# Moving the two normalising activations ahead of the attention-output copy on ScalarE

## The chip, the cores and the metric

The kernel runs on one core of one Trainium2 chip. The metric is the device time of one execution in microseconds (us); lower is better. Engines are called by their short names: PE is TensorE (matmuls, with PEld for the loading of weights), DVE is VectorE, ACT is ScalarE, POOL is GpSimd, SP is SyncE.

## The reference, cut to what matters

A gated cross-attention block followed by a top-1 mixture of experts, over 128 sequences of 128 tokens with 256 features, 16 heads of 16 features, 8 experts:

```python
x = x + tanh(g_xattn[0]) * xattn(layernorm(x), ctx, ctx, bias, ...)   # bias: (128, 16, 128, 128)
x = x + tanh(g_ffn[0])   * ffn(layernorm(x), Wg, bg, W1, b1, W2, b2)

# xattn, one sequence: q, k, v = projections with a low-rank addition
scores = einsum('bqhd,bkhd->bhqk', q * D**-0.5, k) + bias
out = einsum('bhqk,bkhd->bqhd', softmax(scores), v)
# ffn: expert = argmax(x @ Wg + bg); y = gelu(x @ W1[e] + b1[e]) @ W2[e] + b2[e]
```

Each sequence therefore needs two layer norms: one of the input x before the attention, and one of the attention's result (called x2 here) before the expert layer.

## The kernel before, in words

There are two stages. The first works through the 128 sequences, one step k for each, and ends with every token's normalised row scattered to its expert's list in memory. The second runs the expert layer on 72 tiles of 256 tokens. The change lies in the first.

The first stage is a software pipeline written out by hand, separately for each engine. In step k each engine handles several sequences at different ages. The names in the code say which: `nxt` is sequence k+4 (its input is normalised and transposed), `val` k+3 (values), `qry` k+2 and `ky` k+1 (queries and keys, each in every second step for two sequences at once), `cur` k (scores, bias, row maximum), `prev` k-1 (transposing of the scores and the exponentials), `fin` k-2 (probabilities times values, and the output's transpose back), `old` k-3 (second layer norm, transpose of x2), `gate` k-4 and `grp` k-5 (routing, once for four sequences). Eight steps form the body of a hardware loop that runs for k = 16 to 119; the steps before and after are written out.

Each engine executes its instructions in the order in which they are written, and semaphores tie the engines together. In step k:

* PE: scores of `cur` (L464); routing logits in every fourth step (L507); probabilities times values of `fin` into bank 6, `b_x` (L516); eight transposes of `prev` (L479, quarters 0 and 1); then it waits for the copy OT (semaphore `ot_evac`, L529) and transposes OT back (L531); small routing matmuls in some steps (L534, L537, L538); queries or keys (L486), values (L564, L566), the transpose of the normalised x2 (L577), the transposes of the normalised x and of the context (L588, L591) and the other eight transposes of `prev` (L479).
* DVE: in every fourth step `pick_experts` (L863 to L879) and in the step after it `list_slots` (L885 to L891); then two bias additions (L829), a row maximum (L835), two more additions, a second maximum; then, once OT's transpose is done (`o_ready`), the normalisation by the softmax sum, x2 (L928), and the statistics of the two layer norms. The last instruction of the step's statistics is L858 for x2.
* POOL: subtracts the maxima (L381, two a step), and then turns the statistics into a scale and a shift: L400, a power (L402) and two small L407, the first for x, the second for x2. Each L407 signals `shift_ok`. Then it scatters one sequence's rows (L416).
* ACT: the order is that of the diff: in every fourth step the copy LT; the copy OT of bank 6 (L699); the two `normalise` calls (L678, first x2 of `old`, then x of `nxt`), which wait for `shift_ok`; the exponentials of quarters 0 and 1 of `prev` (L685); queries or keys (L658, L669), the copies V (L715), x2T (L721) and XT (L728), and the exponentials of quarters 2 and 3.

The scale and shift that ACT uses in step k come from statistics that DVE finished at the end of step k-1.

I call the four kinds of step by their place in a group of four: A is k mod 4 = 3 (routing logits), B is k mod 4 = 0 (DVE's `pick_experts`), C is 1 (DVE's `list_slots`), D is 2 (nothing extra).

Of the kernel before, what the change touches and what calls it, by code (L numbers as in the profile page):

```python
# [88 lines left out]
def run_steps(eng, first, last, width, loop_rounds, body, heads=None):  # L89

    a, b = loop_rounds
    for s in range(first, a * width):
        body(0, s)
    with eng.bass.Fori(a, b, engines=bass.OrderedEngineSet([eng.engine]), head_slot=heads) as i:
        for k in range(width):
            body(i, k)
    for s in range(b * width, last + 1):
        body(0, s)


def flamingo_block(nc, x, ctx_in, bias, g_xattn, g_ffn, wqT, bq, aq, bqT, wkT, bk, ak, bkT, wvT, bv, av, bvT,
                   wg, bg, w1, w2, b2, consts, row_consts, ids_const, out):
    ctx = ExitStack()
    with ctx:
        def sb(name, shape, dt=F32):
            return ctx.enter_context(nc.sbuf_tensor(name, shape, dt))

        def sem(name):
            return ctx.enter_context(nc.semaphore(name))
# [32 lines left out]
        x_sb = sb("x_sb", [P, 8, HID])  # L142
        ctx_sb = sb("ctx_sb", [P, 4, HID])
        sc = sb("sc", [P, 4, HEADS * P])
        xn = sb("xn", [P, 2, HID])
# [10 lines left out]
        xn2, x2id = x2n[:, :, 0:HID], x2n[:, :, HID]  # L156
        ln = x2n[:, :, HID + 1:HID + 9].rearrange("p t (n c) -> p t n c", c=4)
        x2 = sb("x2", [P, 2, HID])
# [61 lines left out]
        ve_ok, rs_ok, xn_ok, xn2_ok = (sem(t) for t in ("ve_ok", "rs_ok", "xn_ok", "xn2_ok"))  # L220
        shift_ok = [sem(f"shift_ok{i}") for i in range(2)]
        xt_ready, xt_evac = sem("xt_ready"), sem("xt_evac")
# [8 lines left out]
        x2t_ready, x2t_evac = sem("x2t_ready"), sem("x2t_evac")  # L231
# [32 lines left out]
        def seq(i, k, lag):  # L264

            t = At(i, k - lag, U)
            if isinstance(i, int) and not 0 <= i * U + k - lag < N:
                return None
            return t

        def tile(i, k, lag):
            t = At(i, k - lag, FU)
            if isinstance(i, int) and not 0 <= i * FU + k - lag < TILES:
                return None
            return t
# [367 lines left out]
        @block.scalar  # L643
        def _(act):
            for w, wt, a, b in (("v", wvT, av, bvT), ("q", wqT, aq, bqT), ("k", wkT, ak, bkT)):
                act.dma_start(A[w][:], a).then_inc(s_w[w], 16)
                act.dma_start(B[w][:], b).then_inc(s_w[w], 16)
                act.dma_start(W[w][:], wt).then_inc(s_w[w], 16)
            act.wait_ge(s_g, 16 * FIRST_DMAS)
            nc.scalar.activation(tg[:], g_raw[:], ACT.Tanh).then_inc(s_seta, 1)  # L650

            def queries(t):
                pair = t.k // 2 % 2
                if t.reached(4):
                    act.wait_ge(s_ready, t.n(4, -8))
                for o in range(KC):
                    act.wait_ge(q_ready, t.per(2, KC, o + 1))
                    ins = nc.scalar.activation(QT[:, pair, o, :], b_s[o][:, 0:2 * P],  # L658
                                               ACT.Identity, bias=bq_col[:, o:o + 1])
                ins.then_inc(q_evac, 1)  # L660

            def keys(t):
                pair = t.k // 2 % 2
                if t.reached(4):
                    act.wait_ge(s_ready, t.n(4, -8))
                for o in range(KC):
                    act.wait_ge(k_ready, t.per(2, KC, o + 1))
                    for e in range(2):
                        ins = nc.scalar.activation(  # L669
                            KT[:, pair, o, :, e, :], b_s[o][:, 0:2 * P].rearrange("p (s k) -> p s k", s=2),  # L670
                            ACT.Identity, bias=bk_half[:, e, o:o + 1], scale=half_rows[e])
                ins.then_inc(k_evac, 1)

            def normalise(t, n, row, rows, dst, done, turned):
                act.wait_ge(shift_ok[n], t.n(1, 1))
                if t.reached(2):
                    act.wait_ge(turned, t.n(1, -1))
                nc.scalar.activation(dst, rows, ACT.Identity, bias=ln[:, row, n, 1:2],  # L678
                                     scale=ln[:, row, n, 0:1]).then_inc(done, 1)

            def probs(t, q):
                act.wait_ge(tr_ready, t.n(4, q + 1))
                if q == 0 and t.reached(2):
                    act.wait_ge(ot_ready, t.n(1, -1))
                nc.scalar.activation(PT[:, t.slot(2), 512 * q:512 * q + 512], b_t[q % 2][:],  # L685
                                     ACT.Exp).then_inc(pt_ready, 1)

            def step(i, k):
                nxt, val, qry, ky, prev, fin, old, gate = (seq(i, k, lag) for lag in (-4, -3, -2, -1, 1, 2, 3, 4))
                if gate and gate.slot(4) == 3:  # L690
                    act.wait_ge(lt_ready, gate.per(4, 1, 1))
                    if gate.reached(4):
                        act.wait_ge(l_ok, gate.per(4))
                    nc.scalar.copy(LT[:], b_lt).then_inc(lt_evac, 1)
                if fin:
                    act.wait_ge(ot_ready, fin.n(1, 1))
                    if fin.reached(1):
                        act.wait_ge(o_ready, fin.n())
                    nc.scalar.copy(OT[:], b_x[:]).then_inc(ot_evac, 1)  # L699
                if old:  # L700
                    normalise(old, 1, (k - 3) % 8, x2[:, old.slot(2), :], xn2[:, old.slot(8), :], xn2_ok, x2t_ready)
                if nxt:
                    normalise(nxt, 0, (k - 3) % 8, x_sb[:, nxt.slot(8), :], xn[:, nxt.slot(2), :], xn_ok, xt_ready)
                if prev:
                    probs(prev, 0)
                    probs(prev, 1)
                if qry and qry.slot(2) == 0:
                    queries(qry)
                if ky and ky.slot(2) == 0:
                    keys(ky)  # L710
                if val:
                    act.wait_ge(v_ready, val.n(1, 1))
                    if val.reached(8):
                        act.wait_ge(ot_ready, val.n(1, -7))
                    nc.scalar.copy(V[:, val.slot(8), :, 0:D],  # L715
                                   b_v[:, 0:HID].rearrange("p (h d) -> p h d", d=D)).then_inc(v_evac, 1)
                if old:
                    act.wait_ge(x2t_ready, old.n(1, 1))
                    if old.reached(8):
                        act.wait_ge(lt_ready, old.per(4, 1, -1))  # L720
                    nc.scalar.copy(x2T[:, old.slot(8)], b_x2[:, 0:HID].rearrange("p (c t) -> p c t", t=P)  # L721
                                   ).then_inc(x2t_evac, 1)
                if nxt:
                    pair, tok = nxt.k // 2 % 2, P * nxt.slot(2)
                    act.wait_ge(xt_ready, nxt.n(1, 1))
                    if nxt.reached(4):
                        act.wait_ge(k_ready, nxt.per(2, KC, -KC))
                    nc.scalar.copy(XT[:, pair, :, tok:tok + P],  # L728
                                   b_x[:].rearrange("p (c t) -> p c t", t=P)).then_inc(xt_evac, 1)
                if prev:  # L730
                    probs(prev, 2)
                    probs(prev, 3)

            run_steps(act, FIRST, LAST, U, LOOP, step)

            def fstep(i, k):
                t = tile(i, k, -1)
                if t:
                    act.wait_ge(gt_ready, t.n(1, 1))
                    if t.reached(2):  # L740
                        act.wait_ge(h_ready, t.n(1, -1))
                    nc.scalar.copy(xgT[:, t.slot(2)], bank[t.slot(2)][:].rearrange("p (c t) -> p c t", t=FT)  # L742
                                   ).then_inc(gt_evac, 1)
                t = tile(i, k, 0)
                if t:
                    act.wait_ge(h_ready, t.n(1, 1))
                    if t.reached(2):
                        act.wait_ge(y_ready, t.n(1, -1))
                    for o in range(KC):
                        ins = nc.scalar.activation(hT[:, t.slot(2), o, :],  # L750
                                                   bank[2 + t.slot(2)][:, FT * o:FT * o + FT], ACT.Gelu,
                                                   bias=w1_sb[:, t.slot(4), KC * HID + o:KC * HID + o + 1])
                    ins.then_inc(h_ok, 1)

            run_steps(act, FFIRST, FLAST, FU, FLOOP, fstep)
# [326 lines left out]
```

## Time and profile before

| | |
|---|---|
| median of 3 runs | 1427.01 us (1424.8 to 1427.34) |
| the profiled execution: its own time, its span | 1427.01 us, 1424.8 us |
| PE busy | 1359.5 us, 95% |
| PE weight loads busy | 1145.5 us, 80% |
| DVE busy | 1077.0 us, 76% |
| POOL busy | 962.4 us, 68% |
| ACT busy | 895.4 us, 63% |
| granted TensorE clock, mean | 0.981 |

The span runs from the first to the last instruction; the time of a run is 2.2 us longer than it here. The first stage is busy from about 33 us (scores of step 0) to about 1085 us, the expert stage from about 1110 us to the end. In the hardware loop the pattern repeats itself: from the second round on, each round of eight steps lasts 65.4 us to within 0.05 us. Busy time on PE is modelled for each matmul and neighbouring matmuls overlap, so the starts of the groups tell more than the sums.

### The profile page before, as it was taken

The numbers are of one execution on the slowest core, as the hardware profiler recorded it, in microseconds if no ns is written. First come the engines' busy times: TensorE is split into PE (matmuls) and PEld (weight loads), VectorE is DVE, ScalarE is ACT, GpSimd is POOL, SyncE is SP. The second block draws the span as 40 slices with busy tenths as digits, with TensorE's granted clock in tenths as the row PEclk, the third lists the DMA queues.
The fourth block names the chain that finished last, engine by engine and source line by source line (L and its number), as shares of the span: only waits on it lengthen the run. The fifth ranks groups of instructions, "written<-read, shape, count | busy, mean of one in ns | idle before, by whom it ended". The sixth has DMA issues, their size and how long they took to land.

```text
span 1424.8 us, 43541 instructions
## 1 busy us (share of the span) xinstructions
PE 1359.5 (95%) x13462; PEld 1145.5 (80%) x13462; DVE 1077.0 (76%) x2591; ACT 895.4 (63%) x1915; POOL 962.4 (68%) x1062
## 2 busy tenths in 40 slices
PE   6999999999999999999999999999993789999997
PEld 4788888888888888888888888888873678888886
DVE  4899899888889898998898898988996233333333
ACT  2677777777777777777777777777762323333332
POOL 3667777777777777777777777777775234444444
PEclk7999999999999999999999999999996899999999
DMA  7466566665665565666666655666631788888883
GB/s 200 127 171 178 169 187 178 175 187 168 178 187 164 171 191 167 183 183 171 185 173 172 193 164 167 190 172 178 186 106 44 239 248 274 258 260 261 256 254 117
DMA packets 350771, 264.79 MB, mean 186 GB/s; under 512 B 18007, under 2 KB 313335, under 8 KB 350714
## 3 DMA queue, kind: packets, MB, share of 16 engines
q1 hardware_dynamic: 337130, 228.61, 57.5%
q0 software_dynamic: 13056, 34.63, 6.5%
q10 hardware_dynamic: 528, 0.84, 0.2%
q8 instruction: 30, 0.49, 0.1%
q14 instruction: 27, 0.22, 0.1%
HBM read 226.88 MB, written 39.22 MB: 187 GB/s over the span
## 4 chain that ended last, share of the span: by engine, by line
PE 42%; DVE 23%; issue 18%; ACT 9%; POOL 3%; SPq 2%; DMA 1%; DVEq 1%; POOLq 0%; ACTq 0%
DVE sc L829 9%; PE bank L637 8%; PE bank L623 8%; PE bank L479 5%; PE bank L486 5%; ACT PT L685 4%; PE bank L464 3%; PE bank L516 3%; PE bank L566 2%; ACT KT L669 2%; PE bank L612 2%; DVE st L850 2%; DVE x L928 2%; POOL x2n L402 2%; DVE negmax L835 2%
## 5 line engine op out<-in xcount | busy, mean ns | idle before, releaser
L381 POOL TENSOR_TENSOR sc<-sc,negmax 128x1024 f32<-128x1024 f32 x256 | 484.9, 1897 | 126.5 <-DVE negmax L835 122.3
L829 DVE TENSOR_TENSOR sc<-bank,sc 128x512 f32<-128x512 f32 x512 | 328.2, 682 | 49.7 <-PE bank L464 42.8
L835 DVE TENSOR_REDUCE negmax<-sc 128x8 f32<-128x1024 f32 x256 | 312.3, 1220 | 17.0
L685 ACT ACTIVATE PT<-bank 128x512 f32<-128x512 f32 x512 | 277.5, 599 | 0.2
L479 PE MATMUL bank<-cst,sc 128*128 128x128 f32 x2048 | 273.4, 277 | 0.0
L433 POOL DMA_INDIRECT out<-og,ids x144 | 141.7, 984 | 179.3 <-issue 156.5
L479 PEld LDWEIGHTS bank<-cst,sc 128*128 128x128 f32 x2048 | 226.1, 141 | 25.7 <-issue 25.5
L994 DVE SCALAR_TENSOR_TENSOR og<-bank,tg,sc 128x512 f32<-128x512 f32 x72 | 54.1, 751 | 194.2 <-PE bank L637 186.9
L416 POOL DMA_INDIRECT rows_dram<-x2n,slot_i x128 | 138.6, 1083 | 59.1 <-issue 55.2
L699 ACT COPY OT<-bank 128x512 f32<-128x512 f32 x128 | 75.1, 587 | 151.0 <-PE bank L516 151.0
L464 PE MATMUL bank<-KT,QT 32*128 32x256 f32 x2048 | 146.6, 400 | 2.4 <-issue 1.6
L516 PE MATMUL bank<-PT,V 128*32 128x128 f32 x4096 | 138.4, 276 | 6.4 <-ACT PT L685 5.4
L637 PE MATMUL bank<-sc,hT 128*128 128x256 f32 x576 | 144.2, 380 | 0.0
L623 PE MATMUL bank<-xgT,w_sb 128*128 128x256 f32 x576 | 138.0, 383 | 5.4 <-ACT xgT L742 4.4
L516 PEld LDWEIGHTS bank<-PT,V 128*32 128x32 f32 x4096 | 107.1, 110 | 40.4 <-ACT PT L685 36.1
L566 PE MATMUL bank<-wv,XT 128*128 128x256 f32 x512 | 132.6, 382 | 0.0
L486 PE MATMUL bank<-XT,wq 128*128 128x256 f32 x512 | 125.8, 389 | 2.7 <-DVE sc L829 2.0
L486 PE MATMUL bank<-XT,wk 128*128 128x256 f32 x512 | 124.5, 386 | 0.4 <-DVE sc L829 0.4
L669 ACT ACTIVATE KT<-bank,bk_half,cst 128x256 f32<-128x256 f32 x256 | 123.4, 567 | 1.0
L742 ACT COPY xgT<-bank 128x512 f32<-128x512 f32 x72 | 42.1, 585 | 130.0 <-PE bank L612 130.0
L623 PEld LDWEIGHTS bank<-xgT,w_sb 128*128 128x128 f32 x576 | 104.6, 192 | 19.0 <-ACT xgT L742 5.2
L750 ACT ACTIVATE hT<-bank,w_sb 128x256 f32<-128x256 f32 x144 | 60.4, 470 | 91.8 <-PE bank L623 91.8
(134 smaller groups left out, 2217.1 us busy)
## 6 DMA issues: line engine op xcount, KB each, us to landing
sc<-in_bias SPq DMA_DIRECT2D x256, 512.0 KB, 5.0
xg<-rows_dram SPq DMA_DIRECT2D x72, 272.0 KB, 3.6
w_sb<-in_w SPq DMA_DIRECT2D x72, 257.0 KB, 4.1
sc<-in_w SPq DMA_DIRECT2D x72, 256.0 KB
x_sb<-in_x SPq DMA_DIRECT2D x128, 128.0 KB, 2.1
ctx_sb<-in_ctx_in SPq DMA_DIRECT2D x128, 128.0 KB, 4.9
rows_dram<-vacant SPq DMA_DIRECT2D x9, 272.0 KB, 3.1
out<-og,ids POOLq DMA_INDIRECT x144
```

Source lines behind the costliest of these rows:

```text
L381: nc.gpsimd.tensor_tensor(s, s, m, ALU.add).then_inc(sub_ok, 1)
L464: ins = mm(b_s[j][:, 2 * P * c:2 * P * c + 2 * P], QT[rows, pair, c, P * sq:P * sq + P], KT[rows, pair, c, sq].rearrange("p e k -> p (e k) ...
L479: ins = nc.tensor.transpose(b_t[q % 2][:, P * h:P * h + P], sc[:, t.slot(4), o:o + P], ident)
L486: ins = mm(b_s[o][:, 0:2 * P], W[w][:, c, o * P:o * P + P], XT[:, t.k // 2 % 2, first + c, :], start=(c == 0), stop=(c == KC - 1))
L516: ins = mm(b_x[CELL * j:CELL * j + CELL, P * (h // 4):P * (h // 4) + P], V[:, fin.slot(8), h, :], PT[:, fin.slot(2), P * h:P * h + P], sta ...
L566: ins = mm(b_v[:, 0:HID], XT[:, pair, KC + c, tok:tok + P], W["v"][:, c, :], start=False, stop=(c == KC - 1))
L623: ins = mm(bank[2 + t.slot(2)][:, FT * o:FT * o + FT], w1_sb[:, t.slot(4), c * HID + o * P:c * HID + o * P + P], xgT[:, t.slot(2), c, :], ...
L637: ins = mm(y_half, hT[:, t.slot(2), c, a * P:a * P + P], w2_sb[:, t.slot(4), c * HID:c * HID + HID], start=False, stop=(c == KC - 1))
L669: ins = nc.scalar.activation(KT[:, pair, o, :, e, :], b_s[o][:, 0:2 * P].rearrange("p (s k) -> p s k", s=2), ACT.Identity, bias=bk_half[:, ...
L685: nc.scalar.activation(PT[:, t.slot(2), 512 * q:512 * q + 512], b_t[q % 2][:], ACT.Exp).then_inc(pt_ready, 1)
L829: nc.vector.tensor_tensor(s, b_s[q][:], s, ALU.add).then_inc(s_used, 1)
L835: nc.vector.tensor_reduce(negmax[:, t.slot(2), 8 * h:8 * h + 8], sc[:, t.slot(4), 1024 * h:1024 * h + 1024].rearrange("p (h k) -> p h k", ...
```

## The change

In ACT's step the two `normalise` calls are moved from behind the copy OT to ahead of it. Nothing is added or removed: the same instructions with the same waits, in another order on this one engine's queue.

```diff
                 if gate and gate.slot(4) == 3:
...
                     nc.scalar.copy(LT[:], b_lt).then_inc(lt_evac, 1)
+                if old:
+                    normalise(old, 1, (k - 3) % 8, x2[:, old.slot(2), :], xn2[:, old.slot(8), :], xn2_ok, x2t_ready)
+                if nxt:
+                    normalise(nxt, 0, (k - 3) % 8, x_sb[:, nxt.slot(8), :], xn[:, nxt.slot(2), :], xn_ok, xt_ready)
                 if fin:
                     act.wait_ge(ot_ready, fin.n(1, 1))
                     if fin.reached(1):
                         act.wait_ge(o_ready, fin.n())
                     nc.scalar.copy(OT[:], b_x[:]).then_inc(ot_evac, 1)
-                if old:
-                    normalise(old, 1, (k - 3) % 8, x2[:, old.slot(2), :], xn2[:, old.slot(8), :], xn2_ok, x2t_ready)
-                if nxt:
-                    normalise(nxt, 0, (k - 3) % 8, x_sb[:, nxt.slot(8), :], xn[:, nxt.slot(2), :], xn_ok, xt_ready)
                 if prev:
                     probs(prev, 0)
                     probs(prev, 1)
```

## Rows read from the trace of the kernel before

**Rows 1.** Windows: busy PE, PEld, DVE, ACT, POOL; granted clock, DMA share, GB/s.

```profile
617.48:682.87 65.39, 65.03 (x742) 55.16 (x741) 58.70 (x136) 49.29 (x107) 50.53 (x56) 1.00 0.62 177
158.90:160.40 1.50, 0.00 (x0) 0.00 (x0) 0.92 (x6) 0.69 (x2) 1.14 (x3) 1.00 0.55 127
1085.00:1110.00 25.00, 5.01 (x30) 3.54 (x30) 12.65 (x41) 1.24 (x3) 9.48 (x10) 0.50 0.21 69
```

**Rows 2.** Waits in that loop round: total us, times, longest.

```profile
ACT OT L699 <- PE bank L516: 9.2, 8, 1.5
...
PE bank L516 <- ACT PT L685: 0.3, 1, 0.3
```

**Rows 3.** Timeline of PE, one group of four steps: start, duration.

```profile
642.08 1.15 PE L464 MATMUL bank<-KT,QT 32*128 32x256 f32 x16
...
645.53 0.60 PE L531 MATMUL bank<-cst,OT 128*128 128x128 f32 x4
...
650.51 1.15 PE L464 MATMUL bank<-KT,QT 32*128 32x256 f32 x16
...
653.53 0.60 PE L531 MATMUL bank<-cst,OT 128*128 128x128 f32 x4
...
658.74 1.15 PE L464 MATMUL bank<-KT,QT 32*128 32x256 f32 x16
...
661.76 0.60 PE L531 MATMUL bank<-cst,OT 128*128 128x128 f32 x4
...
666.52 1.15 PE L464 MATMUL bank<-KT,QT 32*128 32x256 f32 x16
...
674.43 1.15 PE L464 MATMUL bank<-KT,QT 32*128 32x256 f32 x16
675.50 0.64 PE L507 MATMUL bank<-x2T,wg_pad 128*32 128x128 f32 x16
```

**Rows 4.** Timeline of ACT in two steps of kind C.

```profile
629.43 0.60 ACT L678 ACTIVATE x2n<-x,x2n 128x256 f32<-128x256 f32 x1 [0.62 <-POOL x2n L407]
...
660.96 0.59 ACT L699 COPY OT<-bank 128x512 f32<-128x512 f32 x1 [1.42 <-PE bank L516]
661.79 0.60 ACT L678 ACTIVATE x2n<-x,x2n 128x256 f32<-128x256 f32 x1 [0.24 <-POOL x2n L407]
662.30 0.59 ACT L678 ACTIVATE xn<-x_sb,x2n 128x256 f32<-128x256 f32 x1
662.79 1.05 ACT L685 ACTIVATE PT<-bank 128x512 f32<-128x512 f32 x2
```

**Rows 5.** Timeline of DVE: first additions of a step, last statistics.

```profile
617.27 0.18 DVE L858 BATCH_NORM_AGGREGATE mv<-st 128x2 f32<-128x6 f32 x1
...
620.10 1.29 DVE L829 TENSOR_TENSOR sc<-bank,sc 128x512 f32<-128x512 f32 x2 [0.23 <-DVE CNT L879]
...
627.27 0.18 DVE L858 BATCH_NORM_AGGREGATE mv<-st 128x2 f32<-128x6 f32 x1
...
643.24 1.29 DVE L829 TENSOR_TENSOR sc<-bank,sc 128x512 f32<-128x512 f32 x2 [1.00 <-PE bank L464]
...
650.31 0.18 DVE L858 BATCH_NORM_AGGREGATE mv<-st 128x2 f32<-128x6 f32 x1
...
652.63 0.69 DVE L829 TENSOR_TENSOR sc<-bank,sc 128x512 f32<-128x512 f32 x1 [0.21 <-DVE CNT L879]
...
659.70 0.18 DVE L858 BATCH_NORM_AGGREGATE mv<-st 128x2 f32<-128x6 f32 x1
```

**Rows 6.** Timeline of POOL, the same group: scale and shift.

```profile
661.26 0.50 POOL L407 TENSOR_SCALAR x2n<-x2n,mv 128x1 f32<-128x1 f32 x2 [0.18 <-POOL x2n L402]
```

**Rows 7.** Timeline at the end of the first stage.

```profile
1080.34 0.58 ACT L699 COPY OT<-bank 128x512 f32<-128x512 f32 x1 [1.20 <-PE bank L516]
...
1081.04 0.42 PEld L531 LDWEIGHTS bank<-cst,OT 128*128 128x128 f32 x4 [1.04 <-issue]
...
1087.51 1.08 PE L507 MATMUL bank<-x2T,wg_pad 128*32 128x128 f32 x16 [0.46 <-ACT x2T L721]
```

## The prediction

> **What bounds the kernel now.** I read the windows first. One round of the loop is eight steps in 65.39 us, of which PE is busy 65.03 us; DVE has 58.70, POOL 50.53, ACT 49.29 [rows 1]. Busy time on PE is modelled, so I checked it in the timeline of PE: its groups follow each other without a hole, and the group of four steps from 642.08 to 674.43 takes 32.35 us (8.43 in A, 8.23 in B, 7.78 in C, 7.91 in D) [rows 3]. So PE sets the pace of the first stage, with little to spare. In the list of waits ACT's largest in that round is the one of the copy OT for PE's L516: 9.2 us in eight waits [rows 2]. ACT is idle there, about 1.2 us a step, and that is the hole into which the change could move 1.0 us of work. Whether it can depends on when that work is allowed to start, and on how soon PE wants OT after it. So the views that decide are the timelines of the four engines around one copy.
>
> **What the two sides of the copy allow.** In step C the copy runs from 660.96 to 661.55 [rows 4] and PE starts the transpose of OT at 661.76 [rows 3]. PE would have to wait for a copy that ended later than that, less the hand-over. The hand-over from OT's end to PE is seen where PE did wait: OT ended at 1080.92, PE's weight load began at 1081.04, 0.12 us later [rows 7]. So the copy has 661.76 - 661.55 - 0.12 = 0.09 us of slack.
>
> The `normalise` calls wait for POOL's shift. It was ready only at 661.26 + 0.50 = 661.76 [rows 6], and the first of them started at 661.79, after the copy, having kept ACT idle for 0.24 us; in the C step of the other group it was 0.62 us [rows 4]. They are thus in their present place not late because they stand behind OT, but because of POOL and, ahead of it, DVE.
>
> **The change step by step.** In the new order OT starts behind both. From the end of DVE's last statistics to the first activation: 661.79 - (659.70 + 0.18) = 1.91 us here, and 629.43 - (627.27 + 0.18) = 1.98 us in the other group [rows 4, 5]. Then 0.51 us to the second activation and 0.49 us to the next instruction (here an activation that reads the same kind of bank, so I take it for OT), 0.59 us of the copy [rows 4], and 0.12 us to PE. From the end of the statistics of step k-1 to PE's L531 of step k that makes 3.62 us (3.69 in the other group).
>
> With the statistics where they are now, C's L531 would start at 659.88 + 3.62 = 663.50 instead of 661.76, 1.74 us later; in B at 650.49 + 3.62 = 654.11 instead of 653.53, 0.58 us later [rows 3, 5]. That is a new wait of PE in nearly every step. Behind it on PE's queue stand the projections, the transposes and the next scores; DVE's next additions wait for those scores. The order of ACT's later work hardly matters: the exponentials follow OT by 0.5 us instead of 1.5 us.
>
> The waits don't add up in full, for DVE and POOL gain on a PE that is late. The new pace is that of the longest closed loop of dependences. I follow it through one group, beginning at the late L531 of C:
>
> * PE from L531 of C to the scores of D: 666.52 - 661.76 = 4.76 us [rows 3].
> * PE through D: 7.78 us, taken from C, the step of the same work that did not wait (D's own 7.91 holds a short wait for an exponential) [rows 3].
> * scores of A to DVE's first addition: 643.24 - 642.08 = 1.16 us [rows 3, 5].
> * DVE through A: 643.24 to 650.49, 7.25 us without a hole; `pick_experts` to the first addition of B, 652.63 - 650.49 = 2.14 us; DVE through B to 659.88, 7.25 us [rows 5].
> * hand-over to C's L531: 3.62 us.
>
> Sum: 33.96 us a group, against 32.35 now. In the other group, the one at the start of a loop round, DVE takes 620.10 - 617.45 = 2.65 us for `pick_experts` and 627.45 - 620.10 = 7.35 us for B [rows 5], and the hand-over is 3.69: 34.64 us. The round is then 68.60 us instead of 65.39 [rows 1]: 3.2 us more in eight steps, 0.40 us a step.
>
> Do the other waits add to this loop? Let A start at 0. D took 7.78 us and its statistics ended at most 1.16 + 7.25 us after its start, so 0.63 us into A. A's L531 is then at 0.63 + 3.62 = 4.25 instead of 3.45 (645.53 - 642.08 [rows 3]): up to 0.8 us late. A's statistics end at 8.41. B starts 4.98 us after A's L531 (650.51 - 645.53), at 9.23, and its own L531 could be had 8.41 + 3.62 - 9.23 = 2.80 us into it, before its present 3.02: no wait. B's statistics end at 8.41 + 2.14 + 7.25 = 17.80, C starts at 9.23 + 8.23 = 17.46, and its L531 is 3.96 us into it instead of 3.02: 0.9 us late. The same sum with 2.65, 7.35 and 3.69 gives 1.6 us in the other group. D starts at 26.18, C's statistics end at 17.46 + 1.16 + 7.25 = 25.87 at the latest, and D's L531 is 0 to 0.3 us late; I count nothing for it. So the waits sit in A and C, and the one in A is not on the loop, since DVE doesn't wait for PE in B.
>
> Thirteen rounds of the loop: 13 x 3.2 = 41.7 us. The 24 other steps of the stage have the same order of work; at 0.4 us each 9.6 us. The expert stage is untouched: 0. Total +51 us. Against the profiled execution's own 1427.01 us, which is the median of the runs, that gives 1478 us.
>
> **Bounds.** Low: hand-overs 0.1 us shorter in each group and 0.2 us of DVE's pace gained (1.4 us a group), and nothing in the 24 other steps: 13 x 2.8 = 36, 1463 us. High: each of four hand-overs 0.15 us longer (2.2 us a group) in all 32 groups, 70 us: 1497 us. I take the middle, since every term is a start-to-start distance in the trace. The likeliest case's own range is 1463 to 1497.
>
> **Rivals.** (a) *No catching up.* If every late L531 counted in full, B and C would lose 0.58 + 1.74 = 2.3 us. For D and A I have no such pair of rows; with nothing for them it is 32 x 2.3 = 74 us, with as much again 148 us; I take the upper, as D's statistics follow C's late ones: 1575 us. It needs DVE to be as late as PE at every wait; but DVE takes up OT's transpose only behind its four additions and two maxima, and the loop above shows it running through A and B without PE. Chance 0.04.
>
> (b) *Hidden.* PE's stall is absorbed, no change, 1427 us. That needs a slack of 1 us a step on PE, or statistics that come 0.6 us ahead of every step now; they come 0.02 us ahead of B and 1.14 us after the start of C [rows 3, 5]. Against a slack speaks that PE's starts are dense; for it, that its weight loads fill only 55.16 of 65.39 us [rows 1]. Chance 0.05. The Trainium skill (Perfetto Trace Analysis, Identifying the Most-Contended Engine) says that matmul occupancy does not tell how close TensorE is to its limit and that the busy share of weight loading should be used. By that rule PE has 16% to spare and the sum would be 0 instead of +51; by the dense starts it is +51, and the starts are what the next engine waits for.
>
> (c) *The other side: faster.* Once the activations are out of the way, the exponentials come 1 us sooner behind OT, and PE's wait for them goes: 0.3 us in one step of the round [rows 2] and 0.1 us in D. 0.4 us in 16 rounds' worth of steps is 6 us, 1421 us. It decides if the shift is ready by the time that ACT falls idle, 1.2 us or more before L516 ends, so if the statistics end 0.6 us before each step starts; the rows put them at or after it. Chance 0.03.
>
> (d) *The clock.* The granted clock is 1.00 in the loop and 0.50 between the stages, where PE does 5.01 us of work in 25; a single pause of 1.5 us left it at 1.00 [rows 1]. The new waits are 0.8 to 1.6 us, twice a group. At the lower level, 1.2 GHz, L507 takes 1.08 us instead of 0.64 [rows 3, 7]. If one step in four ran so, 7.8 x 0.69 = 5.4 us a group would come on top: 1478 + 32 x 5.4 = 1651 us. Chance 0.03. The Trainium skill (TensorE: Matmul & The Clock Gate, A second HAM failure mode: psum-queue depth-cycling) tells of a kernel whose frequent short idles between groups made the clock swing between the two levels; by it this case would be the likely one, by the pause in the trace it is not.
>
> **How the numbers follow.** Forecast 0.85, (a) 0.04, (b) 0.05, (c) 0.03, (d) 0.03. A measurement of this kernel can tell 0.2% from no change. Slower holds the forecast, (a) and (d), 0.92; same is (b), 0.05; faster (c), 0.03. The range 1463 to 1497 holds nearly all of the forecast's 0.85, so it stands as it is, with 1460 and 1500 as round ends.
>
> **What the profile would show.** A round of eight steps of 68.6 us. L531 held back by OT in A (up to 0.8 us) and C (0.9 and 1.6 us) and hardly in B and D. ACT's wait of OT for L516 gone, and in its place a wait of the first normalising activation for POOL in every step. DVE waiting for PE's scores in D and A. The clock at 1.00. The prediction is wrong if L531 doesn't wait, if it waits in all four kinds (then (a)), or if the matmuls themselves get longer (then (d)).

## The result and the profile after

The changed kernel takes 1483.49 us (median of 4 runs, 1481.97 to 1484.63) against 1427.17 us for the kernel before beside it. The ratio is 1.0392, 95% interval 1.0377 to 1.0407: 3.9% slower. The forecast was 1478 us, within 1460 to 1500.

| | before | after |
|---|---|---|
| span of the profiled execution | 1424.8 us | 1480.4 us |
| granted TensorE clock, mean | 0.981 | 0.981 |
| one loop round, eight steps | 65.39 us | 68.76 us |
| its steps B C D A, first group | 8.52, 7.95, 8.13, 8.43 | 8.22, 9.56, 7.79, 9.10 |
| its steps B C D A, second group | 8.23, 7.78, 7.91, 8.44 | 8.23, 8.89, 7.84, 9.11 |

The steps are distances between the starts of PE's scores. The windows view of one round of the changed kernel answers to the first row of [rows 1]; columns as there:

```profile
579.15:647.89 68.74, 65.29 (x741) 55.00 (x740) 58.82 (x137) 49.92 (x107) 50.56 (x57) 1.00 0.59 169
```

Every engine does the work it did before; only the length of the round grew, and the clock stayed at 1.00. The waits in the same round (total us, times, longest) answer to [rows 2]:

```profile
ACT x2n L678 <- POOL x2n L407: 6.0, 8, 2.2
DVE sc L829 <- PE bank L464: 5.3, 5, 2.1
...
PE bank L531 <- ACT OT L703: 3.4, 4, 1.6
```

ACT's 9.2 us of waiting for L516 are gone. In their place the first activation waits for POOL's shift, eight times in eight steps, and behind it PE waits for OT in four of the eight: 3.4 us, about what the round grew by. DVE in its turn waits for PE.

The timelines of PE through A, B and C of the second group, and of DVE and ACT in its C (start, duration, the idle time ahead and what ended it) answer to [rows 3, 4, 5]:

```profile
604.72 1.15 PE L464 MATMUL bank<-KT,QT 32*128 32x256 f32 x16
608.78 0.66 PE L531 MATMUL bank<-cst,OT 128*128 128x128 f32 x4 [0.45 <-ACT OT L703]
613.82 1.15 PE L464 MATMUL bank<-KT,QT 32*128 32x256 f32 x16
616.84 0.60 PE L531 MATMUL bank<-cst,OT 128*128 128x128 f32 x4
622.05 1.15 PE L464 MATMUL bank<-KT,QT 32*128 32x256 f32 x16
626.15 0.63 PE L531 MATMUL bank<-cst,OT 128*128 128x128 f32 x4 [0.93 <-ACT OT L703]
630.94 1.15 PE L464 MATMUL bank<-KT,QT 32*128 32x256 f32 x16
```

```profile
622.35 0.18 DVE L858 BATCH_NORM_AGGREGATE mv<-st 128x2 f32<-128x6 f32 x1
```

```profile
624.45 0.60 ACT L678 ACTIVATE x2n<-x,x2n 128x256 f32<-128x256 f32 x1 [1.59 <-POOL x2n L407]
624.95 0.59 ACT L678 ACTIVATE xn<-x_sb,x2n 128x256 f32<-128x256 f32 x1
625.45 0.56 ACT L703 COPY OT<-bank 128x512 f32<-128x512 f32 x1
```

L531 is held in A (4.06 us after the scores instead of 3.45) and in C (4.10 instead of 3.02), and not in B. In C the statistics ended at 622.35 + 0.18 = 622.53 and L531 began at 626.15: 3.62 us, the hand-over of the prediction to the last digit. In the C of the first group L531 is held longest, 4.77 us after the scores instead of 3.02:

```profile
587.37 1.15 PE L464 MATMUL bank<-KT,QT 32*128 32x256 f32 x16
592.14 0.63 PE L531 MATMUL bank<-cst,OT 128*128 128x128 f32 x4 [1.59 <-ACT OT L703]
```

The chain of work that ended last shows the closed loop itself, here from B of the first group into the next A (start, length, engine and line; the longest pieces only):

```profile
578.76 0.20 DVE lmax L863
...
581.70 0.69 DVE sc L829
...
588.27 0.19 DVE mv L858
588.62 0.24 POOL ve L400
588.93 0.73 POOL x2n L402
590.06 0.27 POOL x2n L407
590.95 0.58 ACT xn L678
591.53 0.48 ACT OT L703
592.14 0.63 PE bank L531 x4
592.77 1.73 PE bank L486 x8
...
597.00 1.08 PE bank L464 x16
...
600.12 0.44 PE bank L531 x4
...
604.78 1.11 PE bank L464 x16
...
606.49 0.69 DVE sc L829
```

`pick_experts` and the rest of DVE's B, POOL, ACT, PE's L531 in C, PE through D to the scores of A, and DVE again. The L531 of D (600.12) lies on it as PE's work, not as a wait.

### The profile page after: what moved, and what is told of

The parts are those of the page before. It is cut to its first block, busy times and chain, and to the rows that moved or that the text cites. A ratio compares the mean times of both kernels' runs of the same rounds, so it can differ in the third digit from the quotient of the medians.

```text
span 1480.4 us, 43554 instructions
## 1 busy us (share of the span) xinstructions
PE 1367.4 (92%) x13462; PEld 1144.0 (77%) x13462; DVE 1079.3 (73%) x2591; ACT 904.5 (61%) x1915; POOL 962.8 (65%) x1062
## 4 chain that ended last, share of the span: by engine, by line
PE 48%; DVE 23%; issue 17%; ACT 3%; POOL 3%; SPq 3%; DVEq 1%; DMA 1%; POOLq 0%; ACTq 0%
DVE sc L829 9%; PE bank L486 8%; PE bank L637 7%; PE bank L623 7%; PE bank L479 6%; PE bank L464 5%; PE bank L566 4%; PE bank L531 2%; PE bank L516 2%; DVE st L850 2%; PE bank L612 2%; DVE x L928 2%; POOL x2n L402 2%; DVE negmax L835 2%; DVE CNT L879 2%
## 5 line engine op out<-in xcount | busy, mean ns | idle before, releaser
L416 POOL DMA_INDIRECT rows_dram<-x2n,slot_i x128 | 138.6, 1083 | 59.0 <-issue 55.1
L678 ACT ACTIVATE x2n<-x,x2n 128x256 f32<-128x256 f32 x128 | 77.0, 601 | 106.6 <-POOL x2n L407 105.7
L516 PE MATMUL bank<-PT,V 128*32 128x128 f32 x4096 | 137.6, 275 | 1.8 <-ACT PT L685 1.8
L531 PE MATMUL bank<-cst,OT 128*128 128x128 f32 x512 | 79.7, 278 | 58.0 <-ACT OT L703 58.0
L516 PEld LDWEIGHTS bank<-PT,V 128*32 128x32 f32 x4096 | 106.5, 110 | 33.9 <-ACT PT L685 29.5
```

Source lines behind the costliest of these rows:

```text
L516: ins = mm(b_x[CELL * j:CELL * j + CELL, P * (h // 4):P * (h // 4) + P], V[:, fin.slot(8), h, :], PT[:, fin.slot(2), P * h:P * h + P], sta ...
```

## The experiments

Ratios are against the kernel before on the same chip, whose time there was 1433 to 1436 us; so ratios are compared, not times. The round lengths are the distances between PE's scores in each timeline, once the pattern repeats. They are set beside the 65.39 us of the kernel before, whose only trace comes from the chip of the main comparison, where it took 1427 us; no trace shows its rounds on the chips of the experiments. The new line numbers of the variants are shifted by up to four.

**The wait alone.** Both activations stay behind OT; OT only has to wait for the shift.

```diff
+                if fin and old:
+                    act.wait_ge(shift_ok[1], old.n(1, 1))
                 if fin:
                     act.wait_ge(ot_ready, fin.n(1, 1))
```

> The order of the kernel before, with one wait added: OT waits for the shift of x2 (shift_ok) before it copies; both activations stay behind it. My theory (closed loop PE - DVE A - DVE B - POOL - ACT - PE): the hand-over from the statistics to L531 is 1.91 + 0.59 + 0.12 = 2.62 us, so the groups take 33.0 and 33.7 us, a round of eight steps 66.6 instead of 65.4, in all +19 us: 1446 us (1440 to 1452). Rival W (it is the 1.0 us of ACT's work ahead of the copy that costs, whatever it waits for): nothing, 1427 us. Rival of the first order (each late L531 counts in full, 0.7 us in C and 0.5 in D, none in A and B): also about +20 to +40, so it is told apart by the place: by my theory L531 waits in C alone or nearly so.

Ratio 1.0103 (1.0083 to 1.0122), +15 us (+19 expected); a round 66.65 us, steps of the groups 8.51, 8.88, 7.78, 8.44 and 8.24, 8.57, 7.79, 8.45: only C is longer. The round is as the sum had it (66.6). So a wait without any work moved costs a quarter of the change.

**The work alone.** Two activations of the same size that wait for nothing, at the head of ACT's step.

```diff
+                if fin:
+                    act.wait_ge(s_cst, 16)
+                    for c in range(KC):
+                        nc.scalar.activation(hT[:, 0, c, :], cst[:, 0:FT], ACT.Identity,
+                                             bias=minus_half, scale=minus_half)
                 if gate and gate.slot(4) == 3:
```

> The order of the kernel before, with two additional activations of the same size (128x256, scale and bias from a column) at the head of ACT's step, which wait for nothing and write a buffer that nobody reads in this stage; 2 x 0.5 us more work of ACT ahead of every copy OT. My theory: they fit into the hole in which ACT waits for L516 (1.15 us a step), so nothing: 1427 us (1424 to 1433). Rival W (ACT's work ahead of the copy is the cost): +1 us in every step less what catches up, about as the change itself, 1483 us.

Ratio 0.9997 (0.9987 to 1.0007). 1.0 us more of ACT's work ahead of each of 128 copies costs nothing against the kernel before on the same chip: it fills the idle stretch. That ends the rival W here: what costs is that the work ahead of the copy has to wait for the shift. (Its profiled round was 65.86 us, 0.5 longer than in the trace of the kernel before; more on that below.)

**Each half of the change.** With only the activation for x ahead of OT:

> The other half: only the activation for x stands ahead of OT, the one for x2 stays behind it. Its shift is the first of the two that POOL writes, some 0.25 us earlier. My theory: hand-over 2.87 us, groups 33.2 and 33.9, a round 67.1 us, in all +27 us: 1454 us (1448 to 1460), so less than with x2 alone. Rival W: the same as with x2 alone, 1455 us for both.

Ratio 1.0156 (1.0136 to 1.0177), +22 us (+27 expected), a round 67.13 us, as the sum had it (67.1). With only the one for x2:

> Half of the change: only the activation for x2 stands ahead of OT, the one for x stays behind it. My theory: the hand-over is 1.91 + 0.49 + 0.59 + 0.12 = 3.11 us instead of 3.62, the groups take 33.45 and 34.13, a round 67.6 us, in all +35 us: 1462 us (1457 to 1468), that is clearly more than half of the change's +56. Rival W: half of the change, 1455 us.

Ratio 1.0349 (1.0329 to 1.0370), +50 us. Its rounds are uneven, 67.3 to 70.4 us, with a mean of 68.9; the one read here took 69.41 us where the sum gave 67.6. One activation fewer ahead of OT, and rounds as long as in the full change (68.76). This miss needed a cause of its own. Its timeline, ACT and then PE in a step D, shows it:

```profile
529.02 0.60 ACT L678 ACTIVATE x2n<-x,x2n 128x256 f32<-128x256 f32 x1 [0.64 <-POOL x2n L407]
530.83 0.59 ACT L701 COPY OT<-bank 128x512 f32<-128x512 f32 x1 [1.21 <-PE bank L516]
```

```profile
528.65 1.08 PE L516 MATMUL bank<-PT,V 128*32 128x128 f32 x32
529.66 1.09 PE L479 MATMUL bank<-cst,sc 128*128 128x128 f32 x8
531.47 0.66 PE L531 MATMUL bank<-cst,OT 128*128 128x128 f32 x4 [0.72 <-ACT OT L701]
```

ACT is free from 529.62, L516 ends at 529.73, and OT starts at 530.83: 1.1 us in which nothing that it waits for is open. POOL's row of the same moment:

```profile
529.46 1.08 POOL L416 DMA_INDIRECT rows_dram<-x2n,slot_i  x1 [0.48 <-issue]
```

**Is it the order of OT's waits?** OT waits for two semaphores. In this one the one for `o_ready` is taken at the head of ACT's step, ahead of the activation for x2.

> The kernel with x2's activation alone ahead of OT was 15 us slower than my sum, and its trace shows OT up to 1.1 us after L516 with ACT idle. Here the wait for o_ready stands at the head of the step instead of at OT. If the lateness comes from OT's two waits being taken up one after the other behind the waiting activation, it goes, and the round is 67.6 us (the kernel some +35 us against before). If it is something else, the time stays at about +50 us.

1487.72 us (one run), 53 us above the kernel before beside it, rounds of 69.44 us: the lateness stays, so it is not that.

**The power left out.** On POOL:

```diff
                     nc.gpsimd.tensor_tensor(ln[:, row, a:b, 0], ve[:, a:b], minus_half.broadcast_to([P, b - a]),
-                                            ALU.pow).then_inc(rs_ok, 1)
+                                            ALU.mult).then_inc(rs_ok, 1)
```

> The changed kernel with POOL's power (0.72 us) replaced by a multiplication of the same operands; the output is no longer the reference's, since the layer norm's scale is wrong. It shortens the hand-over by what POOL saves, I expect 0.3 to 0.5 us. My theory: the hand-over is on the closed loop once a group, so a round gets 0.6 to 1.0 us shorter and the kernel 10 to 16 us faster than the changed one: ratio to the kernel before 1.028 to 1.032 instead of 1.039. Rival W (ACT's work is the cost): no gain beyond what the kernel before gains by the same edit.

> The kernel before with the same replacement of the power (output not the reference's, as in the other). My theory: POOL's hand-over is not on PE's path there, only ACT's two waits for the shift in a round get shorter and with them up to 0.4 us of PE's waits a round: ratio 0.996 to 1.000, clearly less gain than in the changed kernel.

POOL's L402 fell from 0.72 to 0.20 us, and both expectations failed: 1.0334 (1.0317 to 1.0350) for the changed kernel, and for the kernel before 1.0201 (1.0184 to 1.0219), 2% slower by doing less. In the first the ratio is lower than the change's 1.0392, but the rounds are not shorter: 68.4 to 69.5 us, 68.9 in the mean, against 68.76. The kernel before was slower on this chip, and that lowers the ratio. The second has the same mark as above: OT up to 1.1 us after L516, now in the old order, with ACT idle for long. The timeline of PE, POOL and ACT in an A:

```profile
596.09 1.06 PE L516 MATMUL bank<-PT,V 128*32 128x128 f32 x32
596.84 1.04 POOL L416 DMA_INDIRECT rows_dram<-x2n,slot_i  x1 [0.39 <-issue]
598.17 0.58 ACT L699 COPY OT<-bank 128x512 f32<-128x512 f32 x1 [1.49 <-PE bank L516]
```

L516 had ended at 597.15, and POOL's scatter had begun 0.31 us before.

I went through OT's copies in all these timelines (those between 160 and 1010 us). A scatter is early if POOL's L416 began more than 0.08 us before L516 ended. A copy is late if it came more than 0.2 us after both L516 and ACT's own last work allowed it. The fifth column counts the clearest cases: ACT was idle and waiting when L516 ended, and the scatter had begun 0.08 to 1.2 us before; the sixth says how many of these copies were late. The last column is the time of the kernel before on the same chip. The wait alone is left out, since its copies wait for the shift too.

| kernel | copies | scatter early | copy late | both | waiting, scatter early | of these late | kernel before there |
|---|---|---|---|---|---|---|---|
| before | 104 | 11 | 0 | 0 | 10 | 0 | 1427 us |
| changed | 99 | 49 | 0 | 0 | 12 | 0 | 1427 us |
| x2 alone ahead | 98 | 50 | 42 | 40 | 17 | 17 | 1434 us |
| x alone ahead | 101 | 2 | 2 | 2 | 2 | 2 | 1434 us |
| work alone | 104 | 25 | 25 | 25 | 25 | 25 | 1434 us |
| x2 alone, `o_ready` first | 98 | 58 | 47 | 47 | 22 | 22 | 1435 us |
| before, no power | 100 | 74 | 65 | 65 | 61 | 61 | 1435 us |
| changed, no power | 98 | 84 | 62 | 62 | 37 | 37 | 1435 us |
| both behind the exponentials (below) | 105 | 1 | 1 | 1 | 1 | 1 | 1435 us |

In the clearest cases the copy was late 165 times out of 165 in seven variants, and 0 times out of 22 in the kernel before and the changed one. That is the split between the chips: these two kernels were profiled where the kernel before takes 1427 us, all variants where it takes 1433 to 1436 us. The split may therefore belong to the chip and not to the kernels. It isn't shown, since neither of the two was profiled on the variants' chips, and no variant on theirs.

A shift that is ready earlier lets the scatter go earlier, and on those chips an earlier scatter goes with late copies. So I tested whether it is their cause.

**The scatter held.** POOL waits for the L516 that OT waits for before it scatters; nothing else changes. (POOL's work behind the scatter moves with it; in the late copy shown above POOL's next work begins only after the copy does.)

```diff
+                    held = seq(i, k, 1)
+                    if held:
+                        pool.wait_ge(ot_ready, held.n(1, 1))
+                        pool.nop(nofuse=True)
                     g, j = t.k // 4 % 2, t.slot(4)
                     nc.gpsimd.indirect_dma_start(
```

> The kernel with x2's activation alone ahead of OT cost 49 us where my sum gave 35, and its trace shows copies OT that start up to 1.1 us after L516 although nothing they wait for is open; that happens where POOL's scatter L416 began before L516 ended. Here POOL waits for L516 of the sequence two behind before it scatters, so that L416 begins only after L516. If the scatter is what delays the copy: no late copies, a round of 67.6 us, ratio to the kernel before 1.024 (1.021 to 1.028). If it is something else: ratio 1.035 as without the hold.

Ratio 1.0222 (1.0205 to 1.0239), a round 67.64 us, no late copy in 100. The windows view of a round, with the hold and without it:

```profile
501.67:569.31 67.64, 65.19 (x741) 54.94 (x740) 58.66 (x136) 49.85 (x107) 50.62 (x57) 1.00 0.60 172
```

```profile
509.61:579.02 69.41, 65.95 (x742) 54.95 (x741) 58.77 (x136) 50.12 (x107) 50.54 (x56) 1.00 0.58 167
```

The sum for this order was 67.6 us. The miss was the scatter's, not the loop's.

> The kernel before without the power (output not the reference's) was 2.0% slower, against my sum; its shift is ready 0.5 us earlier and so is the scatter, which then falls ahead of L516's end. With the scatter held until L516 is done: if the scatter is the cause, ratio 0.996 to 1.001, as my theory had it for this edit; if not, 1.020.

Ratio 0.9889 (0.9872 to 0.9905), a round 64.77 us, no late copy in 105: from 2.0% slower to 1.1% faster with the hold. That the hold removes the loss was expected; that the kernel is faster than 0.996 was not.

> The changed kernel without the power (output not the reference's), scatter held. My theory of the closed loop: the hand-over is 0.52 us shorter (0.20 instead of 0.72 us on POOL) once a group, a round 67.7 instead of 68.76 us, in all 17 us less than the changed kernel: ratio 1.027 (1.024 to 1.030). If the loop were not what sets the pace, no more gain than the kernel before has by the same edit: 1.036 or more.

Ratio 1.0185 (1.0168 to 1.0202), again below the range expected, but a round of 67.60 us (67.7 expected) and no late copy in 101; 1.2 us a round less than the changed kernel's 68.76, against 0.6 us for the same edit in the old order (65.39 to 64.77). So 0.52 us on POOL is worth about twice as much where the loop runs through it. (The changed kernel with the scatter held and the power kept was not run; its trace without the hold has no late copy.)

> Control: the kernel before with nothing but the hold on the scatter. Its scatters begin at or after L516's end already, so ratio 0.998 to 1.002.

Ratio 0.9964 (0.9954 to 0.9974), rounds of 65.4 to 65.5 us. The expectation failed: the hold alone makes the kernel 5.7 us faster than the kernel before on that chip, though its rounds are those of the kernel before on the other chip. It was also wrong on the place of the scatters: in the trace of the kernel before 11 of 104 begin early.

What differs is probably the kernel before itself, from chip to chip. Outside the stretch from the first to the last scores all 14 profiles have 392.5 to 398.0 us. The spans of the kernel before on the chip of the hold have a median of 1433.5 us, so I estimate 1035 to 1041 us for this stretch there, against 1032.0 in its trace and 1032.5 with the hold. Late copies as in the work alone (25 of 104, a round of 65.86 us) would account for that; no trace shows it. By this estimate the ratios of the variants are set against a kernel before that is some 6 us slower than in its trace. For the work alone that leaves a price between nothing and 0.4%, against the 3.9% of the change.

**The other direction.** Both activations behind the exponentials:

```diff
                     nc.scalar.copy(OT[:], b_x[:]).then_inc(ot_evac, 1)
+                if prev:
+                    probs(prev, 0)
+                    probs(prev, 1)
                 if old:
...
-                if prev:
-                    probs(prev, 0)
-                    probs(prev, 1)
```

> The other direction: both activations go behind the exponentials of quarters 0 and 1 (order OT, exponentials, x2, x). My theory: L531 keeps its place, and the two short waits of PE for late exponentials in a round (0.28 and 0.12 us, which come from ACT standing still for the shift in C) go. A round 65.0 us instead of 65.4, in all 16 x 0.4 = 6 us faster than the kernel before on the same chip: ratio 0.9955 (0.993 to 0.998). Rival: the activations now delay the queries or the transposes of x2 and x on PE (L577, L588), then the ratio is over 1.000.

1422.69 us beside 1434.62, ratio 0.9914 (0.9900 to 0.9929), faster than expected and the fastest kernel here that leaves nothing out, a round 64.83 us instead of 65.39. D is 7.78 in both groups; the wait of PE for late exponentials is gone, and the queries and transposes keep their places in their steps to 0.02 us or come earlier. The stretch from the first to the last scores is 7.4 us shorter than in the trace of the kernel before, where 6 were expected. The rest of the 12 is about what the kernel before lost on this chip against its trace; its cause is not shown.

## Why the prediction was right

**The bound and the slack of OT.** Right. PE had no room, and OT no more than 0.1 us: the wait alone, at one place in four, already costs 1.0%.

**The hand-over of 3.62 us.** Right: 3.62 us in the trace after, term by term (1.92 to the first activation, then 0.50, 0.50, 0.56 and 0.14).

**The closed loop.** Right, and supported in three ways: the chain of the changed kernel runs through the engines in that order; four variants with another hand-over (wait alone, x alone, x2 alone with the scatter held, no power with the scatter held) have rounds of 66.65, 67.13, 67.64 and 67.60 us where the sum gave 66.6, 67.1, 67.6 and 67.7; and PE waits in A and C but not in B and D. The waits it forecast were up to 0.8 us in A and 0.9 and 1.6 in C; measured from L531's place they are 0.6, 1.1 and 1.75. From the scores of step 0 to those of step 127 the variants are longer than the kernel before in its trace by 18.7 us (wait alone), 29.3 (x alone), 36.5 (x2 alone, held) and 33.5 (no power, held), where the sums gave 19, 27, 35 and 34. By the ratios it is 15, 22, 32 and 27 us, less by what the kernel before lost on those chips.

**The sum.** A round 68.76 instead of 68.60 us. The 13 rounds together grew by 44.5 us (the first of them by 4.2) instead of 41.7. The 24 other steps: from the scores of step 0 to those of step 127 the stage took 1083.7 us instead of 1032.0, so 51.7 in all and 7.2 for these, where I had 9.6. Before the first scores came another 0.7, and 1.0 from those of step 127 to the first transposes of the expert stage. The expert stage itself, counted at 0, took 317.9 instead of 315.8 us; its length is anything from 315.8 to 319.7 us in the 14 profiles, so those 2 us can't be called a term of the change. The low bound holds a slip: 1.6 less 0.1 and 0.2 is 1.3 us a group and not 1.4, which gives 1461 instead of 1463 us.

**The rivals.** (a) no catching up: refuted, 56 us and not 148, with no wait in B and D. (b) hidden and (c) faster: refuted by the wait of L531. The Trainium skill (Perfetto Trace Analysis, Identifying the Most-Contended Engine) judges TensorE's headroom by the busy share of the weight loads and by the share of the peak arithmetic rate that is reached. The first left 16% here and was no guide to whether a wait is absorbed: the wait alone, which holds L531 in C only, cost 1.0%. The second was not worked out. (d) the clock: 1.00 in the round with two waits of PE, 0.45 to 1.6 us long, in four steps. The swing that the Trainium skill (TensorE: Matmul & The Clock Gate, A second HAM failure mode: psum-queue depth-cycling) tells of does not show here.

**Where it was lucky.** The prediction has no term for POOL's scatter. In the profiled run of the changed kernel none was needed: 49 scatters were early and no copy was late. In the variant with x2 alone, on another chip, late copies made the sum wrong by 15 us. If the difference is the chip's, the changed kernel would cost more there too; it was not run there.

## What to carry to other kernels

An idle stretch on an engine can take work that is ready, not work that must wait: before moving something into it, look at what that something waits for, and when. On an in-order queue the wait moves too, and stands ahead of what was on time. If an engine at its limit is held by such a wait, follow the dependences around until they close and add up that loop from start-to-start distances; it gives the new pace, while adding the single waits does not. Set against the present places of L531 in the trace before, the hand-over makes it late in all eight steps of a round, by 0.3 to 2.1 us and 8.7 us together; the round grew by 3.4.

## What the runs showed of the hardware

A copy on ACT can start up to 1.1 us late although its semaphores' sources are done and ACT is idle, when POOL has begun an indirect scatter (mostly 1.03 to 1.09 us) shortly before the release. It happened in seven variants, in from 1 copy of 105 to 65 of 100, and in none of 410 where the scatter was held back until L516's end. It can turn the saving of 0.52 us of POOL's work into a loss of 2.0%. That the scatter's place is what matters is shown by the hold.

By which path it acts on ACT is open. In the two kernels without the power every late copy that goes with an early scatter starts 1.3 to 1.7 us after the scatter does, in the work alone mostly 0.6 us after it, so no one delay fits all. Open, too, is why the kernel before and the changed one are spared in 22 clear cases of 22. In the changed kernel 12 scatters begin 0.76 us before L516's end with ACT idle for the last 0.10 us of it, and no copy is late. In the variant without the power the same spacing (0.76 to 0.78 us, ACT idle for 0.10 to 0.12) goes with copies 0.7 us late, in 10 cases of 10. The power can't be the reason, since variants that keep it have late copies too. The likeliest difference left is the chip; the changed kernel run on a chip of the variants, or a variant on its own, would decide it. The time of the kernel before, 1427 us on one chip and 1433 to 1436 us on the three others, says how little can be read from times of different chips.
